# Attention and a routed layer on one core: the end of the last pair reordered, its sums shared out anew, shorter roots, a first expert that starts with its high parts

## The reference

```python
# attention, 16 heads of 64
q, k, v = h @ w_q, h @ w_k, h @ w_v
z = softmax(q @ k.T / 8) @ v
x = x + (h + concat(z) @ w_o)              # h = layernorm(x)
# routed layer: 8 experts, each takes at most 512 of the 4096 tokens
probs = softmax(h2 @ Wr)                   # h2 = layernorm(x)
e = argmax(probs); rank = place of the token among those of its expert
y = relu(h2 @ W1[e]) @ W2[e] * probs[e]    # 0 where rank >= 512
x = x + y
```

## Time and profile before

| | us |
|---|---|
| median of 3 runs | 1509.79 (1508.08 to 1510.36) |
| profiled execution | 1508.29 |
| its span, first to last instruction | 1506.2 |
| TensorE busy | 1478.4 (98%) |
| VectorE busy | 995.8 (66%) |
| ScalarE busy | 784.5 (52%) |
| GpSimd busy | 1216.1 (81%) |
| mean granted TensorE clock | 0.995 |

### The profile page before, as it was taken

The page is one execution under the profiler, slowest core; times in us unless marked ns, Lnnn a source line. Parts: engine busy times, 40 slices in busy tenths (PEclk is TensorE's granted clock), DMA queues, the critical chain, the costliest instruction groups (busy, mean ns, idle before and its releaser), DMA issues.

```text
span 1506.2 us, 21680 instructions
## 1 busy us (share of the span) xinstructions
PE 1478.4 (98%) x7244; PEld 841.6 (56%) x7244; DVE 995.8 (66%) x1228; ACT 784.5 (52%) x1540; POOL 1216.1 (81%) x675
## 2 busy tenths in 40 slices
PE   8999999999999999999999999999999999998897
PEld 5555555555555555555555555555655556554586
DVE  6557666676777656766666657676677666677543
ACT  4565556565555554555455555555555455453331
POOL 5888778898798878888778878889789998899535
PEclk9999999999999999999999999999999999999999
DMA  6334444442343434332444433333444423440431
GB/s 149 90 81 93 94 113 108 107 104 60 82 104 88 114 83 108 87 83 65 95 98 100 114 83 90 86 76 89 98 96 96 107 72 79 103 107 12 133 84 34
DMA packets 125294, 137.88 MB, mean 92 GB/s; under 512 B 44107, under 2 KB 69198, under 8 KB 125185
## 3 DMA queue, kind: packets, MB, share of 16 engines
q1 hardware_dynamic: 118784, 130.26, 37.3%
q0 software_dynamic: 2048, 4.10, 0.9%
q10 hardware_dynamic: 4352, 2.13, 0.5%
HBM read 16.81 MB, written 8.45 MB: 17 GB/s over the span
## 4 chain that ended last, share of the span: by engine, by line
PE 87%; POOL 5%; DVE 3%; issue 2%; ACT 1%; SPq 1%; DMA 1%; POOLq 0%; ACTq 0%; DVEq 0%
PE ps_w L1383 27%; PE ps_w L1367 16%; PE ps_w L1368 14%; PE ps_m L1315 10%; POOL acc L662 4%; PE ps_m L1416 3%; PE ps_w L1401 2%; PE ps_m L1283 2%; PE ps_m L1284 2%; PE ps_m L1285 2%; DVE mxw L1054 1%; PE ps_w L1690 1%; DVE z L1068 1%; PE ps_m L1690 1%; PE ps_m L1300 1%
## 5 line engine op out<-in xcount | busy, mean ns | idle before, releaser
L662 POOL TENSOR_TENSOR acc<-acc,ring 128x1024 f32<-128x1024 f32 x382 | 918.9, 2406 | 50.9 <-ACT ring L831 3.3
L1054 DVE TENSOR_REDUCE mxw<-ps_m 128x1 f32<-128x1024 f32 x512 | 601.4, 1217 | 323.3 <-PE ps_m L1315 312.3
L831 ACT ACTIVATE ring<-ps_w 128x512 f32<-128x512 f32 x1024 | 544.8, 600 | 253.5 <-PE ps_w L1368 235.9
L1383 PE MATMUL ps_w<-ring,V 128*64 128x512 f32 x2048 | 467.7, 598 | 0.0
L1367 PE MATMUL ps_w<-queriesA,keysA 128*128 128x512 f32 x1024 | 431.9, 422 | 5.1 <-ACT sums L822 2.8
L1368 PE MATMUL ps_w<-queriesB,keysB 65*128 65x512 f32 x1024 | 406.9, 397 | 0.0
L1383 PEld LDWEIGHTS ps_w<-ring,V 128*64 128x64 f32 x2048 | 135.7, 136 | 265.5 <-issue 234.9
L662 POOL TENSOR_TENSOR acc<-ring 128x1024 f32<-128x1024 f32 x64 | 152.2, 2378 | 157.4 <-PE ps_w L1401 150.5
L1367 PEld LDWEIGHTS ps_w<-queriesA,keysA 128*128 128x128 f32 x1024 | 194.0, 189 | 106.1 <-issue 48.6
L1368 PEld LDWEIGHTS ps_w<-queriesB,keysB 65*128 65x128 f32 x1024 | 194.7, 190 | 33.6 <-issue 0.7
L1315 PE MATMUL ps_m<-keysA,queriesA 64*128 64x512 f32 x1000 | 183.0, 444 | 1.2 <-issue 0.5
(11 more groups left out here) (181 smaller groups left out, 981.3 us busy)
## 6 DMA issues: line engine op xcount, KB each, us to landing
queriesA<-qk_high SPq DMA_DIRECT2D x248, 128.0 KB
keysB<-qk_high SPq DMA_DIRECT2D x124, 128.0 KB
keysA<-qk_rest SPq DMA_DIRECT2D x124, 128.0 KB
queriesB<-qk_rest SPq DMA_DIRECT2D x124, 128.0 KB
by_sums<-sums SPq DMA_DIRECT2D x240, 64.0 KB, 2.0
keysA<-qk_high SPq DMA_DIRECT2D x93, 128.0 KB
tokens_by_slot<-blank ACTq DMA_DIRECT2D x16, 130.0 KB, 3.1
ring<-tokens_by_slot SPq DMA_DIRECT2D x8, 260.0 KB, 5.3
```

Source lines behind the costliest of these rows:

```text
L662: pool.tensor_tensor(acc[h][:, :], before, P_both(kt), ALU.add).then_inc(summed, 1)
L831: act.activation(P_tile(kt, p), ps_s[k % 3][:, :], ACT.Exp, scale=SCALE).then_inc(exp_done, 1)
L1054: dve.tensor_reduce(mxw[h][:, p * HT + qt:p * HT + qt + 1], ps_m[p][:, :], AX_X, ALU.max).then_inc(maxed, 1)
L1383: mm = pe.matmul(ps_z[p * DK:(p + 1) * DK, :], V_of(j, kt, p), P_tile(kt, p), start=(kt == 0), stop=(kt == KT - 1))
```

## The change

The definition of `LAST_BY_PE` goes from 2 to 1, so GpSimd adds one tile more and TensorE sums one less. On VectorE, `scale_z(29, 0)` moves from oct 3 to oct 2 of pair 30; `scale_z(29, 1)` and `scale_z(30, 0)` stay in oct 0 of the last pair but go ahead of the second visit's maxima. The roots take one step of third order and one of second order instead of three Newton steps. At the start `turn_max` goes ahead of `first_visit(4, 0)`. After the last pair `softmax_sums` goes ahead of `count_ranks`. For the first expert alone, the two matmuls with the tokens' high part are issued for three chunks before the wait for the low part; within each chunk the product with the low part now comes last.

```diff
-        LAST_BY_PE = 2
+        LAST_BY_PE = 1
...
-            def newton(v, y, t):
-                then(dve.scalar_tensor_tensor(out=t, in0=y, scalar=-0.5, in1=y, op0=ALU.mult, op1=ALU.mult))
+            def third_order(v, y, t):
+                then(dve.tensor_tensor(t, y, y, ALU.mult))
                 then(dve.tensor_tensor(t, t, v, ALU.mult))
-                return dve.scalar_tensor_tensor(out=y, in0=t, scalar=1.5, in1=y, op0=ALU.add, op1=ALU.mult)
+                then(dve.scalar_tensor_tensor(out=t, in0=t, scalar=-10.0 / 3.0, in1=t, op0=ALU.add, op1=ALU.mult))
+                then(dve.scalar_tensor_tensor(out=y, in0=t, scalar=5.0, in1=y, op0=ALU.add, op1=ALU.mult))
+
+            def second_order(v, y, t):
+                left = 3.0 / 8.0
+                then(dve.scalar_tensor_tensor(out=t, in0=y, scalar=-0.5 * left ** 3, in1=y, op0=ALU.mult, op1=ALU.mult))
+                then(dve.tensor_tensor(t, t, v, ALU.mult))
+                return dve.scalar_tensor_tensor(out=y, in0=t, scalar=1.5 * left, in1=y, op0=ALU.add, op1=ALU.mult)
...
-                for _ in range(3):
-                    then(newton(v, y, t))
+                third_order(v, y, t)
+                then(second_order(v, y, t))
...
-                then(newton(v, y, t))
-                then(newton(v, y, t))
+                third_order(v, y, t)
...
-                newton(v, y, t).then_inc(root_ready, 1)
+                second_order(v, y, t).then_inc(root_ready, 1)
...
+                    if last and oct == 0:
+                        scale_z(j - 2, 1)
+                        scale_z(j - 1, 0)
                     if oct == 2 and not (first or last or both):
                         recip(j - 1, 1, 3)
                     if not (last and oct >= 1):
...
                         reduce_max(v, h, qt, 1)
                         reduce_max(v, h, qt, 0)
-                    if oct == 0 and last:
-                        scale_z(j - 2, 1)
-                        scale_z(j - 1, 0)
-                    if oct == 3 and known(j, LAST - 1):
+                    if oct == 2 and known(j, LAST - 1):
                         scale_z(j - 1, 0)
...
-            first_visit(4, 0)
             pe.wait_ge(first_copied, 4)
             turn_max(0, 0, ps_z)
+            first_visit(4, 0)
...
+            softmax_sums(LAST, 1, LAST_BY_PE)
             count_ranks(B - 1, lent_out)
-            softmax_sums(LAST, 1, LAST_BY_PE)
...
+            def up_by_high(e, c):
+                n, w = e * FC + c, slice(e * F + c * P, e * F + (c + 1) * P)
+                if n >= 3:
+                    pe.wait_ge(relu_done[(n - 3) % 2], (n - 3) // 2 + 1)
+                pe.matmul(up_bank(n), w1_low[:, w], xeT_high[e % 2][:, :], start=True, stop=False)
+                pe.matmul(up_bank(n), w1_high[:, w], xeT_high[e % 2][:, :], start=False, stop=False)
+
+            def up_by_low(e, c):
+                n, w = e * FC + c, slice(e * F + c * P, e * F + (c + 1) * P)
+                pe.matmul(up_bank(n), w1_high[:, w], xeT_low[e % 2][:, :], start=False,
+                          stop=True).then_inc(up_done, 1)
+
             for e in range(E):
+                ahead = 3 if e == 0 else 0
+                pe.wait_ge(xeT_split, e + 1)
+                for c in range(ahead):
+                    up_by_high(e, c)
                 pe.wait_ge(xeT_ready, e + 1)
                 for c in range(FC):
...
+                    if c >= ahead:
+                        up_by_high(e, c)
+                    up_by_low(e, c)
```

## The result

| | before | changed | ratio, 95% interval |
|---|---|---|---|
| first comparison, median us | 1508.93 (6 runs) | 1503.93 (6 runs) | 0.9963 [0.9952, 0.9975] |
| once more (e9 below) | 1508.52 (20 runs) | 1503.95 (8 runs) | 0.9972 [0.9960, 0.9985] |
| profiled executions | 1508.29 | 1504.45, later 1503.36 | |

The account below looks back on a forecast made before the run. TensorE, 87% of the chain, was taken as the bound, with time won where it waits or runs at low clock. 5.2 - 0.4 + 0.4 + 0.4 + 0.1 = 5.7 us gave 1502.6, median 1503.3; range 1500.3 to 1506.6 us.

Parts of the forecast that it names:

- Scaling of z: Around the last pair: moving three scalings removes two TensorE waits and a half-clock stretch, together 5.6 us earlier.
- One more tile: Last sums: TensorE saves 0.9 us but waits 1.6 us for GpSimd; sums start 5.2 us earlier, not 6.8.
- Ranks behind the sums: After the last pair: ranks end 0.3 us behind the sums, VectorE reads them later, the reciprocal follows; cost 0.4 us.
- At the end, first half: hidden behind the wait for the logits: VectorE's first-half root after the pairs: its shortening is hidden by the wait for the logits, so no gain counted.
- Roots: VectorE's roots in two steps; at the start two instructions fewer before the first product, 0.4 us, 0 if weights came late.
- Second half of the end: VectorE's second-half root after the pairs: six instructions become four, choosing starts with the logits; gain 0.4 us.
- First expert: TensorE starts high parts 0.7 us sooner, but the fourth chunk waits for relu; 0.1 us is left, 0 to 0.6.
- first turn: At the start, turn ahead of a visit: first scores wait for another visit, so nothing, 0.2 us either way.
- B: Rival, 15%: GpSimd not late before the last sums, 1.6 us more, and less low clock: 1500.3 to 1501.7 us.
- D: Rival, 12%: last pair's two scalings stay slow, maxima come late and the clock falls: 1505.3 to 1506 us.
- E: Rival, 4%: clock stays at half from the new wait until tokens are turned, 12.3 us; slower, 1514.9 us.
- C: Rival, 17%: TensorE's new wait before the last sums lowers the clock earlier, about 3 us: 1505.6 to 1506.5 us.

Follow-up runs that it names:

- e9: The changed kernel run again unaltered, on one chip with three other runs; 1503.95 us, 0.9972 of the kernel before.
- e4: The kernel before with only the three scalings of z moved; 1502.51 us, 0.9954 of the kernel before.
- e11: The kernel before with only the three scalings of z moved, run again beside the whole change; 1503.86 us, 0.9963 of the kernel before.
- e2: The changed kernel with the three scalings of z back in their old places; 1507.59 us, 0.9993 of the kernel before.
- e1: The changed kernel with two tiles of the last sums on TensorE again; 1502.10 us, 0.9953 of the kernel before.
- e8: The changed kernel with one operand of the last pair's first-half root in PSUM and two tiles on TensorE; 1504.29 us, 0.9963 of the kernel before.
- e10: The changed kernel with one operand of the first half's root in PSUM, ranks ahead of the sums and two tiles on TensorE; 1501.86 us, 0.9959.
- e6: The changed kernel with one operand of the last pair's first-half root in PSUM, by three Newton steps; 1504.57 us, 0.9959 of the kernel before.
- e12: The changed kernel with 8 spare products ahead of the last sums and 8 ahead of the first half's ranks; 1504.56 us, 0.9974 of the kernel before.
- e5: The changed kernel with the edits to the first turn and the first expert undone; 1505.08 us, 0.9965 of the kernel before.
- e3: The changed kernel with three Newton steps for VectorE's roots as before; 1505.24 us, 0.9976 of the kernel before.

## Why the prediction was right, and where it was not

**Scaling of z, 5.6 us: right in each term.** By the marks the sums' first products come 5.76 us sooner (56.91 to 51.15), made of the two waits and the half-clock stretch: 1.3, 2.9 and 1.6 us by the starts in between, where 1.1, 2.9 and 1.6 were forecast. The two scalings among the scatters took 1.5 us of the forecast 1.4 to 2.5, the third 2.21 of the 2.75 us that were free, and TensorE waited for none. e4 and e11 show that this edit by itself gives as much as the whole change, e2 that without it the time can't be told from before.

**One more tile, "worth nothing": it costs.** The prediction's own numbers said so: with two tiles TensorE would start the sums at 1411.7, with one GpSimd lets it at 1412.4, a loss of 0.7 us; by the marks it is 0.3 us (52.94 in e1, 53.23 and 53.28). GpSimd ended at 1412.46 against 1412.4. Measured from the mark that is 53.2 against 53.9 (one scatter stretched by 0.3 us, not two by 0.9 together), while TensorE arrived at 52.2 against 52.3: it waited 1.0 us, not 1.6. But the adds don't only end late, they hold VectorE: e1 is 1.3 us sooner at the reciprocal than the same kernel with the extra tile (e9), and at w1 too.

**Ranks behind the sums, 0.4 us: the step that was mis-sized.** From the last sums to the reciprocal the gain falls from 5.8 to 4.0 us (4.6 in e9): 1.8 and 1.2 us instead of 0.4. The order by itself is not the reason: where no one-hot matrix is late, the reciprocal follows the start of the sums by 2.65 us with the ranks behind (e1, e8) and by 2.47 with the ranks ahead (before, e10), 0.2 us. The failed assumption stands under the roots, "At the end, first half: hidden behind the wait for the logits". It took the root's 0.2 us steps from a place where GpSimd was idle and did not ask what would run beside the first half's root once the scalings were out of the way. e6 shows the cause (no wait with one operand in PSUM), e1 and e4 where it comes from.

**Roots.** Start: forecast 0.4 us. By the timelines the first products start at 10.75 to 11.00 us in eight of ten profiles with the new roots (11.16 and 11.27 in two), and at 11.16 to 11.38 in four with Newton's: 0.3 to 0.4. At the mark nothing of it can be seen: of the seven profiles at full clock up to there, the six with the new roots pass it at 1358.10 to 1358.74, the one with Newton's (before) at 1358.50. Second half of the end: forecast 0.4 us. From the reciprocal to the second one-hot matrix it takes 6.69 us before. Only e10, with 6.28, shows the 0.4. In e1, e2, e8, e9 and e12 it is 6.51 or 6.52, half of the forecast, since one instruction beside a scatter took 0.41 us instead of 0.17; and it is 7.19 in the changed kernel's first profile, where half clock made the logits the late ones (VectorE waits 0.85 us for them).

**First expert 0.1 us, first turn nothing:** as measured by e5 (0.11 and nothing).

**The rivals.** B did not come: GpSimd was late. D did not: the scalings were cheap. E did not. C is half true. In five profiled executions TensorE waits about 1 us for GpSimd ahead of the sums (changed, e9, e3, e5, e6); in four of them the half clock stayed for 10.2 us or more, in e9 it didn't. Of the nine others none had more than 6.8 us. So the wait for GpSimd goes along with the long half clock in four profiles of five, and that is a risk and not a constant cost: 1.3 us where it came in the changed kernel, against the 3 of the rival. That the wait brings it about is not shown. Why it falls one way or the other in two executions of one kernel stays open; e5, which has the changed kernel's code from the mark to w1, had 17.1 us.

**The sum.** By e9's profile, w1 starts 4.8 us sooner from the mark (68.51 to 63.72) where 5.2 were forecast, and by the first profile 3.5. With the start's 0.3 to 0.4 this is 3.8 to 5.2 us; medians and ratios say 4.2 to 5.6. The spans close with two shares that are not put down to an edit: the mark itself came 0.8 us later (e9: 1.2), with 3.4 us at half clock in the first 60 us (e9: 6.8) where the profile before had none, and from w1 to the end it took 78.2 us (e9: 78.0) where it took 79.2. So 3.5 - 0.8 + 1.0 = 3.7 us, and 4.8 - 1.2 + 1.2 = 4.8, the differences of the spans. The part from w1 on varies by 1.6 us among ten profiles with the same code there (78.0 to 79.6), and with the old order for the first expert it took 77.9 to 79.4 in four, so only 0.1 of its gain, the first expert's, is charged to the change. That the forecast landed so close is in part luck: the ranks cost 0.8 to 1.4 us more than forecast and the second root gave 0.2 us less in most profiles, while GpSimd was 0.7 us less late.

## What to carry to other kernels

When an edit moves work earlier, list what runs on the other engine at the new time, for small instructions too: their price in the old place holds only for the old neighbours. Before handing an idle engine more work, ask whom it blocks while it works, not only when it ends. An edit made of six parts can owe all of its gain to one; run that one alone.

## What was not expected of the hardware

- A VectorE instruction on 128x4 numbers with two inputs in SBUF that started just behind the start of one of GpSimd's adds (about 2.35 us) lasted 2.25 to 2.27 us, until 0.02 us behind the add's end, in all eight profiles with such an instruction; otherwise it took 0.16 us. With one of the inputs in PSUM such instructions took 0.15 to 0.17 us beside the same adds. The one behind each long one took 0.16 us; it started in the 0.15 us between two adds or after the last.
- The root's first instruction, with one input in SBUF and its result there, took 0.70 to 1.92 us beside the adds (1.92 in e2) and ended with an add each time; 0.16 us without them, 0.15 us with its result in PSUM (e6). So two inputs in SBUF are not the only case that waits.
- Two profiles of one kernel had stretches at half clock of 13.6 and 6.8 us after the last pair, 1.28 us apart at w1. Differences of 1 us between single profiles say little unless the stretches are compared as well.
